# An adaLN block on one core: raw first keys, the scale in column blocks, first keys and values by pairs, and statistics spread by TensorE

## What is computed

```
mod = (silu(c) @ wmod).reshape(4, 6, 1, 1024)      # sa, ca, ga, sb, cb, gb
h = layernorm(x) * (1 + ca) + sa
q, k, v = split(h @ Wqkv + bqkv)                   # 256 columns each
x = x + ga * (softmax(q @ k.T / 16) @ v @ Wo + bo)
h = layernorm(x) * (1 + cb) + sb
x = x + gb * (h @ weight.T + bias + lora(h))
```

## Time and profile before

| | us |
|---|---|
| median of 3 runs | 1042.85 |
| lowest and highest | 1041.23, 1042.93 |
| the profiled execution | 1042.57 |
| its span, from the first to the last record | 1040.8 |
| TensorE busy | 1011.5 (97% of the span) |
| VectorE busy | 663.6 (64%) |
| ScalarE busy | 309.2 (30%) |

### The profile page before, as it was taken

The page is one execution under the profiler, slowest core; times in us unless marked ns, Lnnn a source line. Parts: engine busy times, 40 slices in busy tenths (PEclk is TensorE's granted clock), DMA queues, the critical chain, the costliest instruction groups (busy, mean ns, idle before and its releaser), DMA issues.

```text
span 1040.8 us, 12891 instructions
## 1 busy us (share of the span) xinstructions
PE 1011.5 (97%) x5158; PEld 831.6 (80%) x5158; DVE 663.6 (64%) x827; ACT 309.2 (30%) x460; POOL 231.2 (22%) x182
## 2 busy tenths in 40 slices
PE   4899999999999999999999999999999999999996
PEld 1677777888888889888898888888887888888885
DVE  4866756498744398532976548776688578566622
ACT  1422333123232132420234523322432333142300
POOL 0000000423201322004230034342223315042411
PEclk9899999999999999999999999999999999999999
DMA  9987574767102553024443146565553646463421
GB/s 348 409 317 244 211 295 140 252 227 265 70 1 77 207 197 127 1 94 157 155 162 117 41 142 225 203 220 184 200 202 126 216 145 202 140 225 122 142 76 66
DMA packets 54475, 180.74 MB, mean 174 GB/s; under 512 B 5784, under 2 KB 6352, under 8 KB 54416
## 3 DMA queue, kind: packets, MB, share of 16 engines
q1 hardware_dynamic: 45152, 146.35, 40.9%
q0 software_dynamic: 9104, 33.04, 8.4%
q10 hardware_dynamic: 160, 0.53, 0.1%
HBM read 146.25 MB, written 33.65 MB: 173 GB/s over the span
## 4 chain that ended last, share of the span: by engine, by line
PE 91%; DMA 4%; DVE 2%; SPq 1%; issue 1%; POOL 0%; ACT 0%; DVEq 0%; POOLq 0%; ACTq 0%
PE pairC L1370 8%; PE pairA L1370 8%; PE pairC L1371 8%; PE pairC L1372 7%; PE pairA L1371 7%; PE pairA L1372 7%; PE pairD L1370 7%; PE pairD L1371 7%; PE pairD L1372 7%; PE pairB L1370 5%; PE pairB L1371 5%; PE pairB L1372 5%; DMA z_cols<-in_x_cols 2%; PE pairB L1526 1%; PE pairD L1478 1%; PE pairA L1478 1%
## 5 line engine op out<-in xcount | busy, mean ns | idle before, releaser
L923 POOL TENSOR_TENSOR xr<-xr,row_bc 128x1024 f32<-128x1024 f32 x32 | 79.9, 2503 | 110.1 <-DMA xr<-in_x 90.3
L936 POOL TENSOR_TENSOR res<-res,row_bc 128x1024 f32<-128x1024 f32 x32 | 81.7, 2565 | 83.4 <-DMA res<-x_dram 76.9
L1370 PE MATMUL pairC<-w_hi,h_hi 128*128 128x512 f32 (+1 forms) x256 | 90.1, 352 | 0.0
L1371 PE MATMUL pairC<-w_lo,h_hi 128*128 128x512 f32 (+1 forms) x256 | 90.0, 351 | 0.0
L1372 PE MATMUL pairC<-w_hi,h_lo 128*128 128x512 f32 (+1 forms) x256 | 89.6, 350 | 0.0
L1370 PE MATMUL pairD<-w_hi,h_hi 128*128 128x512 f32 (+1 forms) x224 | 77.6, 346 | 0.0
L1371 PE MATMUL pairD<-w_lo,h_hi 128*128 128x512 f32 (+1 forms) x224 | 77.6, 346 | 0.0
L1372 PE MATMUL pairD<-w_hi,h_lo 128*128 128x512 f32 (+1 forms) x224 | 77.2, 345 | 0.0
L928 POOL DMA_DIRECT2D x_dram<-xr x32 | 18.0, 562 | 229.3 <-DVE xr L1276 229.3
L1079 ACT ACTIVATE w_hi<-w_sum 128x1024 fp32r<-128x1024 f32 x32 | 33.8, 1059 | 100.5 <-DVE w_sum L1320 100.2
L1370 PE MATMUL pairB<-w_hi,h_hi 128*128 128x512 f32 (+1 forms) x160 | 59.8, 374 | 0.0
(11 more groups left out here) (344 smaller groups left out, 2570.9 us busy)
## 6 DMA issues: line engine op xcount, KB each, us to landing
wm<-in_wmod SPq DMA_DIRECT2D x48, 512.0 KB, 6.4
xr<-in_x SPq DMA_DIRECT2D x34, 512.0 KB, 4.0
z_cols<-in_x_cols SPq DMA_DIRECT2D x32, 512.0 KB, 6.3
x_dram<-xr POOLq DMA_DIRECT2D x32, 512.0 KB, 3.8
xs<-x_dram SPq DMA_DIRECT2D x32, 512.0 KB, 4.7
w2t<-in_w2t SPq DMA_DIRECT2D x32, 512.0 KB, 4.3
res<-x_dram SPq DMA_DIRECT2D x32, 512.0 KB, 5.7
out_y<-res POOLq DMA_DIRECT2D x31, 512.0 KB, 3.5
```

Of the source, the lines that this page charges most:

```text
L923: nc.gpsimd.tensor_tensor(xt, xt, row_bc[:, :], ALU.add).then_inc(residual_made, 1)
L936: nc.gpsimd.tensor_tensor(rt, rt, row, ALU.add).then_inc(residual2_made, 1)
L1370: nc.tensor.matmul(out, left[0], right[0], start=first, stop=False)
L1371: nc.tensor.matmul(out, left[0], right[1], start=False, stop=False)
```

## The change

1. The first modulation vector, `ca`, is computed in four blocks of 256 columns. `Lwm (0, k)` loads 512 rows by 256 columns: eight DMAs as before, of 512 KB each, but in runs of 1 KB and not of 4 KB. `M0 (c)`, `MC0`, `MT0`, `MM0` replace `M (0, r)`, `MC`, `MT`, `MM` for it, and `HH` of the first chunk waits for its own block alone.
2. `K0 (c)` alternates with a new `V0 (c)`, which does the values of the first chunk from the same two channel tiles. `PARTS` has the value weights before the query weights.
3. The statistics of both chunks of batch 0 are spread by TensorE: `BCM (j)` for the mean, `BCP (j)` for one over the deviation. ACT copies both from `pairA` into `bc` (`BMC`, `BPC`), and `Z` reads them there. `RT0`, `SC`, `SW` and `LBC` of the second chunk go.
4. Keys of batch 0 leave PSUM without bias (`KR`, into the new tile `k_raw`); `KH` and `KL` read `k_raw` later.
5. The silu of `c` stands ahead of the statistics on DVE. Tiles of `wmod` are used four in turn instead of six from the second vector on. All five tables are written anew.

```
-PARTS = ((1, 0), (1, 1), (0, 0), (0, 1), (2, 0), (2, 1))
+PARTS = ((1, 0), (2, 0), (1, 1), (2, 1), (0, 0), (0, 1))
...
+    ("BCM", (0,), "A", None), ("BCP", (0,), "A", None), ("M0", (0,), "B", None), ("MT0", (0,), "B", None),
+    ("M0", (1,), "C", None), ("MT0", (1,), "C", None), ("K0", (0,), "D", None), ("M0", (2,), "A", ("BCM", 0)),
+    ("V0", (0,), "B", ("M0", 0)), ("K0", (1,), "D", None), ("M0", (3,), "C", ("M0", 1)), ("MT0", (2,), "A", None),
+    ("V0", (1,), "B", None), ("MT0", (3,), "C", None), ("BCM", (1,), "A", ("M0", 2)), ("K0", (2,), "D", None),
+    ("BCP", (1,), "A", None), ("V0", (2,), "B", None), ("M", (1, 0), "C", ("M0", 3)), ("M", (1, 1), "C", None),
+    ("K0", (3,), "D", None), ("V0", (3,), "B", None), ("Q", (0, 0, 0), "A", ("BCM", 1)), ("M", (1, 2), "C", None),
...
         def wm_slot(n):
-            return n if n < 8 else (n - 8) % 6 if n < 16 else n % 4
+            return n if n < 8 else n % 4
...
                     q = MOD_COLUMN[s]
-                    sp.dma_start(wm[wm_slot(n)][:, :], wmod[k * P:(k + 1) * P, q * H:(q + 1) * H]).then_inc(
+                    if s == CA:
+
+                        half, at = k % 2, q * H + k // 2 * 2 * P
+                        src = wmod[half * BANK:(half + 1) * BANK, at:at + 2 * P].rearrange("(k p) n -> p k n", p=P)
+                        sp.dma_start(wm[k].rearrange("p (k n) -> p k n", k=4), src).then_inc(ld_wm[k], 16)
+                        return
+                    sp.dma_start(wm[wm_slot(n)], wmod[k * P:(k + 1) * P, q * H:(q + 1) * H]).then_inc(
...
+                elif what == "MC0":
+                    c = i[0]
+                    act.wait_ge(mod_used, 2 * c + 2)
+                    wait(act, ca_turned, c - 1)
+                    nc.scalar.activation(mod_rows[:, c % 2 * 2 * P:(c % 2 + 1) * 2 * P], ps[:, 0:2 * P], ACT.Copy).then_inc(ca_copied, 1)
+                elif what in ("BMC", "BPC"):
+
+                    j = i[0]
+                    if what == "BMC":
+                        act.wait_ge(mean_spread, j + 1)
+                    else:
+                        act.wait_ge(stat_spread, j + 1)
+                    wait(act, z_made, 4 * j)
+                    cols = slice(0, CHUNK) if what == "BMC" else slice(CHUNK, 2 * CHUNK)
+                    nc.scalar.activation(bc[:, cols], ps[:, cols], ACT.Copy).then_inc(spread_copied, 1)
...
                     act.wait_ge(z_made, 8 * b + 4 * j + k + 1)
-                    act.wait_ge(mod_made, 1)
+                    act.wait_ge(ca_made, k + 1 if b + j == 0 else 4)
...
+                elif what == "KR":
+
+                    _, j, m = i
+                    act.wait_ge(k_done, 2 * j + m + 1)
+                    act.wait_ge(mod_used, 6)
+                    nc.scalar.activation(k_raw[:, m, j * CHUNK:(j + 1) * CHUNK], ps[:, m * BANK:(m + 1) * BANK],
+                                         ACT.Copy).then_inc(k_raw_made, 1)
...
+                elif what == "M0":
+
+                    c = i[0]
+                    if c == 0:
+                        pe.wait_ge(c_ready, 1)
+                    for k in range(CT):
+                        if k % 4 == 0:
+                            pe.wait_ge(ld_wm[2 * c + k // 4], 16)
+                        q = 32 * (k % 4)
+                        last = nc.tensor.matmul(ps[q:q + 32, 0:2 * P], scT[:, k * B:k * B + 32],
+                                                wm[2 * c + k // 4][:, k % 4 * 2 * P:(k % 4 + 1) * 2 * P],
+                                                start=(k < 4), stop=(k >= 4))
+                        if k % 4 == 3:
+                            last.then_inc(mod_used, 1)
...
+                elif what == "V0":
+
+                    c = i[0]
+                    pe.wait_ge(w_lo_made, PARTS.index((2, c // 2)) + 1)
+                    pe.wait_ge(h0_lo_made, 2 * c + 2)
+                    for ct in range(2 * c, 2 * c + 2):
+                        for t in range(4):
+                            last = product3(ps[:, t * D:(t + 1) * D], both(h_hi[0], h_lo[0], ct, slice(t * P, (t + 1) * P)),
+                                            both(w_hi, w_lo, ct, slice(2 * D, 3 * D)), ct == 0 and t % 2 == 0, ct == CT - 1)
+                    if c == 3:
+                        last.then_inc(v_done, 2)
```

More of the change, by code:

```diff
@@ L521, in build_block @@
             with ExitStack() as early:
-                wm = [sb(f"wm{i}", [P, H], at=early) for i in range(4)]
+                wm_pair = [sb(f"wm{i}", [P, 2, H], at=early) for i in range(2)]
             wo_hi = sb("wo_hi", [P, DT, H], F32R, at=first)
@@ L709, in wait_emptied @@
             if what == "M":
-                eng.wait_ge(mod_made, i[0] + 1)
-            elif what == "BCP":
-                eng.wait_ge(z_made, 4)
+                eng.wait_ge(mod_made, i[0])
+            elif what == "M0":
+                eng.wait_ge(ca_made, i[0] + 1)
+            elif what == "BCM":
+                eng.wait_ge(spread_copied, 2 * i[0] + 2)
             elif what == "WU":
@@ L726, in wait_emptied @@
                 eng.wait_ge(q_lo_made, 4 * i[0] + 2 * i[1] + 2)
+            elif what == "K" and i[0] == 0:
+                eng.wait_ge(k_raw_made, 2 * i[1] + 2)
             elif what == "K":
@@ L961, in step @@
                     act.wait_ge(mod_used, CT * (s + 1))
-                    wait(act, mod_turned, s)
+                    if s == SA:
+                        act.wait_ge(ca_turned, 4)
+                    else:
+                        act.wait_ge(mod_turned, s - 1)
                     if s == GA:
@@ L1229, in step @@
                     dve.wait_ge(hi_made, 4 * b + 2 * j + m + 1)
-                    nc.vector.scalar_tensor_tensor(lo[where], ps[:, m * BANK:(m + 1) * BANK],
+                    src = k_raw[where] if what == "KL" and b == 0 else ps[:, m * BANK:(m + 1) * BANK]
+                    nc.vector.scalar_tensor_tensor(lo[where], src,
                                                    bias_qkv[:, col + m, b:b + 1], hi[where].bitcast(F32),
@@ L1369, in product3 @@
             def product3(out, left, right, first, last):
-                nc.tensor.matmul(out, left[0], right[0], start=first, stop=False)
-                nc.tensor.matmul(out, left[0], right[1], start=False, stop=False)
-                return nc.tensor.matmul(out, left[1], right[0], start=False, stop=last)
+                nc.tensor.matmul(out, left[0], right[0], start=first, stop=False, skip_group_check=True)
+                nc.tensor.matmul(out, left[0], right[1], start=False, stop=False, skip_group_check=True)
+                return nc.tensor.matmul(out, left[1], right[0], start=False, stop=last, skip_group_check=True)
             def both(hi, lo, *where):
@@ L1405, in step @@
                     last.then_inc(mod_turned, 1)
-                elif what == "BCP":
+                elif what in ("BCM", "BCP"):
+                    j = i[0]
                     pe.wait_ge(ld_const, 16)
-                    pe.wait_ge(rstd_made, 1)
-                    for k in range(2):
-                        for t in range(4):
-                            at = k * CHUNK + t * P
-                            last = nc.tensor.matmul(ps[:, at:at + P], stat[:, 0, k, t:t + 1].to_broadcast([P, P]), ident,
-                                                    start=True, stop=True)
-                    last.then_inc(stat_spread, 1)
+                    if what == "BCM":
+                        pe.wait_ge(stat_made, 4 * j + 4)
+                    else:
+                        pe.wait_ge(rstd_made, j + 1)
+                    k = 0 if what == "BCM" else 1
+                    for t in range(4):
+                        at = k * CHUNK + t * P
+                        last = nc.tensor.matmul(ps[:, at:at + P], stat[:, j, k, t:t + 1].to_broadcast([P, P]), ident,
+                                                start=True, stop=True)
+                    last.then_inc(mean_spread if what == "BCM" else stat_spread, 1)
                 elif what == "RT0":
@@ L1494, in step @@
                     if b == 0:
-                        pe.wait_ge(w_lo_made, 4 if what == "Q" else 2)
+                        pe.wait_ge(w_lo_made, 6 if what == "Q" else 4)
                     at = (0 if what == "Q" else D) + m * P
```

136 lines of the change are left out of this document (77 added, 59 removed), and 679 rows, old and new, of tables (ACT_ORDER, DVE_ORDER, PE_ORDER, POOL_ORDER).

## The result

| | before | with the change |
|---|---|---|
| median us | 1042.03 (20 runs) | 1048.5 (20 runs) |
| lowest, highest | 1040.75, 1043.67 | 1039.16, 1051.2 |
| ratio of the two, 95% interval | | 1.0045 [1.0027, 1.0063] |

The change makes the kernel slower, by 0.45% (a ratio of all runs; the medians lie 0.6% apart), where I forecast 1039.8 us. But no single time is behind that median. Five of the 20 runs took 1039.2 to 1040.9 us, one 1043.8, and fourteen 1047.8 to 1051.2: a **lower group** and an **upper group**, 9 us apart. Before had one group, 3 us wide.

A forecast was written before the change was run, and what follows sets the result against it. TensorE, busy 1011.5 of 1040.8 us, was taken as the bound, with loads binding the start. 1042.57 - 1.4 (start) - 1.7 (second clock fall) = 1039.5 us profiled; median 0.28 above, 1039.8; range 1037.7 to 1043.2.

The forecast's parts named there:

- a microsecond saved before 58 us is one off the end: From `K0 (0)` at 30.60 us on, TensorE is fed almost without gap, so early savings reach the end unless it starves later.
- a wait of over 1 us appears after 60 us: Sign in TensorE's waits after 60 us that would show the forecast of 1039.8 us to be wrong.
- slower rival: At `M (1, 1)`, 1 KB packets land the 34th load after 52.0 us and the clock falls again; up to 1045.1 us, chance 0.12.
- Statistics at 14.8, `K0 (0)` at 24.7: At the head, statistics end at 14.8 us, not 12.1; TensorE starts `K0 (0)` at 24.7, 5.9 us earlier.
- the 2.7 us charged to the silu: At the head on DVE, the silu ahead of the statistics makes them end at 14.8 us, not 12.1: 2.7 us lost.
- 34th load at 50.6: The load that `M (1, 1)` needs lands at 50.6 us: 49.15 plus 1.5 for eight loads in 1 KB runs.
- my 0.18: Extra cost of 1 KB runs: 0.18 us for each of the eight loads, 1.5 us in all.
- 49.15: Landing in us of the 34th load if all loads are as fast as before: 24.81 + 19 x 1.281.
- `M (1, 1)` ends at 51.1: TensorE's matmuls end 0.5 us after the 34th load, at 51.1 us; bounds 49.7 and 53.0; start gains 1.4 us.
- break-even of 52.5: End of `M (1, 1)` at 52.5 us would mean no change: 52.30 + 0.22, as the work left behind it differs.
- One stretch at half clock before 35 us, none from 60 to 130: Granted clock falls once in the start; the second fall, at 83.6 us, goes: 1.7 us gained.
- The sum, 1039.5 for the profiled execution: Whole kernel: 1042.57 less 1.4 us from the start and 1.7 from the second clock fall gives 1039.5 us.

The follow-up runs named there:

- r2: The change with the eight loads of `ca` in runs of 4 KB, laid out by the host, not 1 KB; ratio 1.0057 to before.
- r6: The change with `RS2 (4)` ahead of `R2 (0,1,0,0)`, `NM (4)` ahead of `FG (0,1,0,0)`, store `YS (0,1,0,1)` ahead of two additions; median 1039.5 us, ratio 0.9988.
- r8: r6 with the silu's DVE operations back behind the four statistics; median 1039.4 us, ratio 0.9983 to before.
- r7: r6 with the eight loads of `ca` in runs of 4 KB, laid out by the host; median 1037.6 us, ratio 0.9966 to before.
- r1: The change once more, nothing edited, profiled in the upper group; ratio 1.0045 to before.
- r3: The change with only `RS2 (4)` moved ahead of `R2 (0,1,0,0)` on POOL; median 1044.2 us, ratio 1.0022 to before.
- r4: The change with store `YS (0,1,0,1)` ahead of two additions, breaking POOL's row of three; median 1043.1 us, ratio 0.9997 to before.
- r10: The change with POOL's store `YS (0,1,0,0)` one place later, behind addition `R2 (0,1,0,1)`; ratio 1.0050 to before.
- r12: The change with stores `YS (0,1,0,0)` and `YS (0,1,0,1)` behind POOL's three additions; ratio 1.0028 to before.

## Why the prediction was wrong, step by step

**The step that failed** is the sentence that TensorE is fed almost without a gap from 30.60 us to the end, so that a microsecond saved before 58 us is one off the end, *as long as TensorE is not starved later*. My terms end at 87 us, and I costed nothing behind that. The condition was the whole case: rewritten orders of POOL and DVE at 675 to 690 us starve TensorE for 7.5 us and cost 2.9 more by the clock, in the profiled execution of the upper group, to which 22 of 32 runs of the change belong. The sentence that the forecast is wrong if a wait of over 1 us appears after 60 us named the sign; no rival had that place or price. My slower rival, the 1 KB loads, was another mechanism: r2 has the upper group without them, r6 has none with them.

**The terms of the sum**, read in the lower group:

- *Statistics at 14.8, `K0 (0)` at 24.7.* Measured 14.64 and 24.53. Right. But the 2.7 us charged to the silu cost the end nothing (r8), which agrees with my saying that the load binds.
- *34th load at 50.6.* Measured 52.09, past the 52.0 that I had named as the sign of the slower rival; its 0.5 us at `M (1, 1)` came too, its further fall of the clock did not. The price of 1 KB runs was nearly right: r7 ends `M (1, 1)` 1.7 us ahead of the change and 1.9 ahead of r6, 0.21 to 0.23 us a load against my 0.18. The landings say the same: each of the eight loads lands 1.46 to 1.50 us behind the load before it in the change, and 1.27 to 1.29 in r7. What was off is the base: with 4 KB runs it still lands at about 51.47 - 1.05 = 50.4, where I had 49.15. Of these 1.2 us 0.7 were to be had from the trace of before, where the same load lands at 49.83: I carried 1.281 us a load on from 24.81, but two loads at 41.7 and 44.7 us landed 1.6 and 1.7 us behind the ones before them. In r7 one lands 2.82 us behind (32.21 to 35.03), though the queue moved 408 GB/s and 1.13 MB in that time, over twice the bytes of a load; whose bytes these are is open. The page "DMA: Bandwidth & Descriptors" of the Trainium skill ("Specifications") has 512 B and more at line rate. The windows from 14 to 24 us speak against that for 1 KB, first the change, then r7. The estimate from the three cycles a packet of the same page of the Trainium skill ("Why small descriptors are slow"), 0.09 us a load, is under half of what was measured:

```profile
14.00:24.00 10.00, 7.54 (x52) 5.10 (x52) 4.96 (x9) 3.31 (x8) 2.03 (x2) 1.00 1.07 372
```
```profile
14.00:24.00 10.00, 7.53 (x52) 5.09 (x52) 4.97 (x9) 3.29 (x8) 2.02 (x2) 1.00 1.03 413
```

- *`M (1, 1)` ends at 51.1.* Measured 53.14: 1.5 us from the landing, and 1.05 us and not 0.5 for the last four matmuls, a time that stood in the earlier trace rows (four of them at 24.81 us). By my own break-even of 52.5 the start **lost** 0.6 us instead of gaining 1.4. The forecast of the mechanism, load and not TensorE, was right.
- *One stretch at half clock before 35 us, none from 60 to 130.* Both as forecast: 1.7 us.
- *The sum, 1039.5 for the profiled execution.* It took 1039.47. That is luck: -0.6 + 1.7 = 1.1 us are explained by my terms, and 3.1 came. The other 2.0 are waits that before had after 58 us, on which I had put no price. The largest is a load of modulation weights at 122 us, which the merged row hides (eight such matmuls take 1.07 elsewhere):

```profile
122.27 2.17 PE L1395 MATMUL pairC<-wm,pads 128*32 128x512 f32 x8
...
  DMA wm<-in_wmod: 1.0, 1
```

The 0.6 us behind `probs` of the earlier trace rows went as well; smaller waits after 58 us add up to 0.8 us in both kernels. That leaves 0.3 to 0.4 us that I did not place.

**Why the change made two groups.** The row of the DMA queue that holds the load of `R2 (0,1,0,0)` starts at 668.2 us in both profiles of the change, but the load lands at 673.0 in one and at 675.3 in the other. Seven profiles have `NM (4)` in the change's place. The four with a landing at 674.7 to 675.3 (r1, r3, r4, r10) are of an upper group; in the three with 671.0 to 673.0 (the change, r2, r12) both halves took 0.81 us. In r3, r4 and r10 the load is also issued later, at 669.4 to 669.7 us, since the store of `out_y` that its tile waits for landed later. Why it takes 2.4 us longer in r1, issued at the same time, is open. Before, `RS2 (4)` and `NM (4)` stood ahead of that load's addition, so its landing did not matter.
